# A graph network's gated layer: its steps one longer, three buffers each, and the gathered rows added by VectorE

## The chip, the cores and the metric

The kernel runs on one core of a Trainium2 chip. The metric is the device time of one execution in microseconds (us), the median of several runs. Engines: PE (TensorE), VectorE (DVE), ScalarE (ACT), POOL (GpSimd) and SP (SyncE); the last two mostly issue DMAs.

## The reference

Four graph layers follow one another on 6250 nodes of 128 features, over 106250 edges sorted by the node they point to. Each layer takes `h = relu(layernorm(x))`, and its result is added to `x`: an attention layer, a sum scaled by degrees, a gated layer, and a mean with two weight matrices. The change touches the gated one:

```
x_row, x_col = x[row], x[col]                       # row: source of an edge, col: its target
gates = sigmoid(x_row @ W_src + x_col @ W_dst + edge_attr @ W_edge)
messages = (x_row @ W_msg) * gates
out = segment_sum(messages, col) / maximum(segment_sum(gates, col), 1e-6)
out = out + (x @ W_root + b_root) + x
```

## The kernel before, in words

Edges are cut into tiles of 128 (each tile holds targets of one block of 128 nodes), and four tiles make a group; 220 groups are live. A stage is written as a loop over steps, unrolled by hand, and each engine's program has its own loop with its own offsets: step i of an engine may work on group i for one part and on group i-1 or i-2 for another. Each engine takes its instructions in the order in which they are written, and semaphores tie the engines together. There is no scheduler.

The gated stage, for group q, before the change:

- POOL gathers 128 rows for each tile, four gathers, from the table `tab2` into slot q mod 4 of `G2`. A row holds `x_row @ W_src` (columns 0 to 127) and `x_row @ W_msg` (128 to 255), made in the stage before. From the fifth group on it waits until the product of group q-4 is done (`gated["multiplied"]`), line 820.
- SP loads an index row (`RELROW`, line 910) and four tiles of transposed edge features (`EA`, line 913, a ring of four).
- ScalarE makes from the index row the one-hot rows `ST` (lines 1417, 1419), one step ahead, in two buffers.
- PE, in step q: edge features by `W_edge` (line 1255), one-hot rows by the block's `x_col @ W_dst` (line 1259), and the gathered `x_row @ W_src` added in the same PSUM bank by a product with the identity matrix (line 1263), whose end signals `pre_done`. Then, of group q-1, the aggregation: one-hot matrix `S` by gates and messages `RHS` (line 1047, shared by all layers), signal `agg_done`.
- ScalarE takes the sigmoid of the PSUM bank into `RHS` (line 1426), signal `gate_done`.
- VectorE, in step q: the one-hot matrix `S` of q (line 1579), the product of gates and gathered rows of q-1 (line 2192), signal `multiplied`, and the four additions of q-2 from PSUM into the node sums (line 1598). The index of the block to add to is read into a register first.

Every four groups one block of nodes is finished ("a turn"): VectorE divides, adds and takes moments in a few short instructions, ScalarE takes a square root and normalises the rows, SP stores them.

Of the kernel before, what the change touches and what calls it, by code (L numbers as in the profile page):

```python
# [12 lines left out]
P = 128  # L13
# [8 lines left out]
RING = 4  # L22
DEEP = 8
# [63 lines left out]
def build(nc, sz, a):  # L87
# [4 lines left out]
    with ctx:  # L92
# [333 lines left out]
        hist_in = sem("hist_in")  # L426
        table_made = sem("table_made")
        table_out = sem("table_out")
        srow_in = sem("srow_in")
# [290 lines left out]
        gated = {k: sem(k + "_gated") for k in ("far_known", "st_made", "pre_done", "gate_done", "multiplied")}  # L720
        rel_loaded = [sem(f"rel_loaded{r}") for r in range(2)]
        ea_loaded = [sem(f"ea_loaded{r}") for r in range(RING)]
# [29 lines left out]
        RELROW = SCR[:, 0:512].bitcast(BF16).rearrange("p (r e) -> p r e", r=2)  # L752
        EA = SCR[:, 1024:3072].rearrange("p (r j e) -> p r j e", r=RING, j=QUAD)
# [150 lines left out]
        def sp_edge_rows(sp):  # L904

            def step(i, u):
                q, slot, turn, v = at(i, u, 0)
                if live(q):
                    wait(sp, gated["st_made"], q - 1)
                    sp.dma_start(RELROW[:, v % 2, :], reld.rearrange("(q r) e -> q (r e)", r=QUAD)[bass.ds(q, 1), :]  # L910
                                 .to_broadcast([P, QUAD * P])).then_inc(rel_loaded[v % 2], 16)
                    for j, first in enumerate(registers(sp, SROW, q, sz.edge_end)):
                        sp.dma_start(EA[:, slot, j, :], a["ea_t"][:, bass.ds(first, P)]).then_inc(ea_loaded[slot], 16)
# [3 lines left out]
                due_now = turn_at(i, u, 10)  # L917
# [5 lines left out]
            steps(sp, step, after(10))  # L923
# [52 lines left out]
        def _(sp):  # L976
# [45 lines left out]
            with nc.allow_non_contiguous_dma(reason="single words"):  # L1022
                for m in range(PARTS):
                    run = slice(m * GROUP * sz.chunk, (m + 1) * GROUP * sz.chunk)
                    sp.dma_start(SROW[:, run].rearrange("o (t g) -> o t g", t=GROUP),
                                 metad[1:2, run].rearrange("o (g t) -> o t g", t=GROUP)).then_inc(srow_in, 16)
            sp.wait_ge(srow_in, 16 * PARTS)
# [115 lines left out]
        def _(pe):  # L1143
# [103 lines left out]
            def step(i, u):  # L1247
                q, slot, turn, v = at(i, u, 0)
                if live(q):
# [3 lines left out]
                    pe.wait_ge(ea_loaded[slot], (turn + 1) * 64)  # L1253
                    for j in range(QUAD):
                        nc.tensor.matmul(QD[v % 2][:, j, :], EA[:, slot, j, :], W[:, 4 * D:5 * D], start=j == 0, stop=False,  # L1255
                                         skip_group_check=True)
                    pe.wait_ge(s["st_made"], q + 1)
                    for j in range(QUAD):
                        nc.tensor.matmul(QD[v % 2][:, j, :], ST[:, v % 2, j, :],  # L1259
                                         QT[:, bass.ds(blocks[j], 1), :].rearrange("p o d -> p (o d)"), start=False, stop=False,  # L1260
                                         skip_group_check=True)
# [7 lines left out]
            steps(pe, step, 1)  # L1269
# [6 lines left out]
        def _(act):  # L1276
# [136 lines left out]
            def spread_rows(q, turn, v):  # L1413

                act.wait_ge(rel_loaded[v % 2], (turn + 1) * 16)
                far = RELROW[:, v % 2, :]
                nc.scalar.activation(far, far, ACT.Square, bias=minus_p).then_inc(s["far_known"], 1)
                act.wait_ge(s["far_known"], q + 1)
                nc.scalar.activation(ST[:, v % 2, :, :].rearrange("p j e -> p (j e)"), far, ACT.Relu, bias=1.0, scale=-1.0
                                     ).then_inc(s["st_made"], 1)  # L1420
# [907 lines left out]
```

## Time and profile before

| | |
|---|---|
| runs | 5820.23, 5826.75, 5829.6 us, median 5826.75 |
| profiled execution | 5859.65 us, its span 5858.1 us |
| mean granted clock of TensorE | 0.70 |
| busy over the span | PE 54%, VectorE 53%, ScalarE 23%, POOL 58% |
| DMA | 615.68 MB, mean 105 GB/s |

The span is from the first to the last instruction. Busy shares are averages over stages with different limits: attention, degrees, gated, mean. The gated stage lies between about 3170 and 4610 us. An engine's idle time is put down to the instruction or DMA that released it; "remote" stands where the releaser has no name in the profile, "issue" where the engine waited for nothing that the profile shows.

### The profile page before, as it was taken

To read this page: it belongs to the slowest core of one execution; us is meant where nothing else is said; L and a number is where in the kernel's file an instruction comes from. 1 tells how busy PE (TensorE), PEld (TensorE's weight loads), DVE (VectorE), ACT (ScalarE), POOL (GpSimd) and SP (SyncE) were. 2 spreads that over 40 slices of the span, in tenths; PEclk is the share of its full clock that TensorE was granted. 3 is DMA by queue.
4 is the path that set the end of the run, shared out by engine and by line. 5 is a ranking of instruction groups with operands and counts; after the bars stand their busy time and mean duration, and the time that the engine had idled before them with its cause. 6 is when DMAs were issued, how large, how long until landed. Compare 5 with 4: busy or idle time off the path is not lost.

```text
span 5858.1 us, 61960 instructions
## 1 busy us (share of the span) xinstructions
PE 3148.9 (54%) x15785; PEld 2606.2 (44%) x15785; DVE 3122.3 (53%) x8346; ACT 1366.9 (23%) x2626; POOL 3380.4 (58%) x3531
## 2 busy tenths in 40 slices
PE   6445445454562444444445777777777445433334
PEld 4344444444452333333334666666666334323333
DVE  6556566656676555544444555555555345443334
ACT  2222222222211000001112434434434111111112
POOL 2466556665513666666663555565665466666664
PEclk8666677766775555566767988898998655565555
DMA  3466666666721111112224555555555411111111
GB/s 88 129 172 183 177 184 186 184 187 185 175 60 47 46 46 46 47 52 57 57 57 86 147 143 143 146 146 142 148 147 142 68 48 48 49 49 49 49 48 39
DMA packets 533610, 615.68 MB, mean 105 GB/s; under 512 B 95885, under 2 KB 418126, under 8 KB 533264
## 3 DMA queue, kind: packets, MB, share of 16 engines
q0 software_dynamic: 141168, 347.22, 22.7%
q1 hardware_dynamic: 392096, 264.52, 17.2%
q8 instruction: 136, 2.23, 0.2%
q14 instruction: 210, 1.72, 0.1%
HBM read 527.32 MB, written 84.05 MB: 104 GB/s over the span
## 4 chain that ended last, share of the span: by engine, by line
another core or an unknown queue 26%; DVE 23%; PE 20%; issue 18%; DVEq 5%; ACT 5%; POOL 1%; DMA 1%; SPq 1%; ACTq 0%; POOLq 0%
DVE ACCR L1598 10%; PE PSA L1047 7%; PE PB L1263 3%; PE PB L1255 2%; PE PB L1259 2%; PE PB L615 2%; DVEq L765 2%; DVE SCR L1521 1%; PE PB L1200 1%; ACT FLG L1426 1%; DVEq L1598 1%; DVE S L1579 1%; DVE SCR L2102 1%; DVE FLG L2192 1%
## 5 line engine op out<-in xcount | busy, mean ns | idle before, releaser
L820 POOL DMA_INDIRECT G<-tab,SRC x2640 | 2540.1, 962 | 1784.5 <-issue 765.9
L1598 DVE TENSOR_TENSOR ACCR<-ACCR,PSA 128x128 f32 (+2 forms) x3488 | 1113.9, 319 | 1307.0 <-remote 809.3
L1047 PE MATMUL PSA<-G,S 128*128 128x128 f32 x3326 | 736.8, 390 | 488.1 <-DVE S L1579 283.0
L884 POOL DMA_INDIRECT G<-tab,MV x783 | 741.5, 947 | 384.3 <-issue 221.3
L1047 PEld LDWEIGHTS PSA<-G,S 128*128 128x128 f32 x3326 | 648.7, 289 | 552.0 <-issue 537.5
L1047 PE MATMUL PSA<-FLG,S 128*128 128x256 f32 x1760 | 517.5, 446 | 298.9 <-DVE FLG L2192 268.8
L1047 PEld LDWEIGHTS PSA<-FLG,S 128*128 128x128 f32 x1760 | 373.1, 219 | 503.0 <-DVE FLG L2192 355.1
L1200 PE MATMUL PB<-QTR,ST 128*128 x1792 | 370.6, 370 | 341.9 <-DVE SCR L2089 214.8
L1200 PEld LDWEIGHTS PB<-QTR,ST 128*128 128x128 f32 x1792 | 324.9, 270 | 379.2 <-issue 378.0
L1579 DVE TENSOR_TENSOR S<-PB,REL 128x512 f32<-128x512 f32 x664 | 455.0, 685 | 6.5 <-DMA MV<-mvd 0.7
L2192 DVE TENSOR_TENSOR FLG<-G,FLG 128x512 f32<-128x512 f32 x220 | 151.7, 689 | 465.4 <-ACT FLG L1426 346.4
L1047 PE MATMUL PSA<-SCR,S 128*128 128x137 f32 x1792 | 354.9, 359 | 14.0 <-DVE SCR L2102 14.0
L1047 PEld LDWEIGHTS PSA<-SCR,S 128*128 128x128 f32 x1792 | 331.0, 265 | 23.4 <-DVE SCR L2102 20.6
L1426 ACT ACTIVATE FLG<-PB 128x512 f32<-128x512 f32 x220 | 130.2, 592 | 702.3 <-PE PB L1263 399.2
L1255 PEld LDWEIGHTS PB<-W,SCR 128*128 128x128 f32 x1760 | 275.5, 223 | 39.9 <-issue 16.8
L1121 PE MATMUL PB<-SCR 128*128 128x50 bf16 x880 | 79.0, 216 | 380.7 <-issue 229.4
L1255 PE MATMUL PB<-W,SCR 128*128 128x128 f32 x1760 | 271.4, 304 | 18.2 <-issue 15.2
L1121 PEld LDWEIGHTS PB<-SCR 128*128 128x128 bf16 x880 | 51.2, 115 | 428.2 <-issue 253.9
L1259 PE MATMUL PB<-QTR,ST 128*128 x1760 | 241.0, 281 | 0.0
L1109 PE MATMUL PB<-W,SCR 128*128 128x512 f32 x114 | 95.0, 928 | 248.7 <-ACT SCR L1321 220.1
L1263 PE MATMUL PB<-G,ident 128*128 128x512 f32 x440 | 227.9, 599 | 0.8 <-issue 0.8
L1259 PEld LDWEIGHTS PB<-QTR,ST 128*128 128x128 f32 x1760 | 225.7, 200 | 0.0
(415 smaller groups left out, 4214.5 us busy)
## 6 DMA issues: line engine op xcount, KB each, us to landing
mvd<-G SPq DMA_DIRECT2D x224, 256.0 KB
MV<-mvd SPq DMA_DIRECT2D x224, 256.0 KB
SCR<-in_ea_t SPq DMA_DIRECT2D x880, 64.0 KB
G<-tab,SRC POOLq DMA_INDIRECT x2640
S<-relt SPq DMA_DIRECT2D x224, 128.0 KB
SCR<-reld SPq DMA_DIRECT2D x220, 128.0 KB
G<-tab,MV POOLq DMA_INDIRECT x783
tab<-SCR SPq DMA_DIRECT2D x57, 128.0 KB
```

The costliest lines, as they stand in the source:

```text
L820: nc.gpsimd.indirect_dma_start(out=rows[:, slot, j, :], out_offset=None, in_=table, in_offset=bass.IndirectOffsetOnAxis(ap=SRC[:, k:k + 1] ...
L884: nc.gpsimd.indirect_dma_start(out=whole_rows(q, j), out_offset=None, in_=tab1, in_offset=bass.IndirectOffsetOnAxis(ap=SRCALL[:, k:k + 1], ...
L1047: last = nc.tensor.matmul((PSA if banks is None else banks)[:, par, j, 0:width], S[:, slot, j, :], rhs(j), start=True, stop=True)
L1121: nc.tensor.matmul(HISTP, LOH[:, (2 * v + k) % (2 * RING), j, :], HIH[:, (2 * v + k) % (2 * RING), j, :], start=first, stop=final, skip_gr ...
L1200: last = nc.tensor.matmul(QD[v % 2][:, j, :], ST[:, v % 2, j, :], QT[:, bass.ds(blocks[j], 1), :].rearrange("p o d -> p (o d)"), start=Tru ...
L1255: nc.tensor.matmul(QD[v % 2][:, j, :], EA[:, slot, j, :], W[:, 4 * D:5 * D], start=j == 0, stop=False, skip_group_check=True)
L1259: nc.tensor.matmul(QD[v % 2][:, j, :], ST[:, v % 2, j, :], QT[:, bass.ds(blocks[j], 1), :].rearrange("p o d -> p (o d)"), start=False, sto ...
L1263: nc.tensor.matmul(QD[v % 2], ident[:, :], G2[:, slot, :, 0:D], start=False, stop=True, skip_group_check=True).then_inc(s["pre_done"], 1)
L1426: nc.scalar.activation(RHS[:, v % 2, :, D:2 * D], QD[v % 2], ACT.Sigmoid).then_inc(s["gate_done"], 1)
L1579: return v_.tensor_tensor(S[:, slot, :, :], bc(IOTAP, [P, QUAD, P], 1), rel[:, bass.ds(q * QUAD, QUAD)].unsqueeze(2).to_broadcast([P, QUAD ...
L1598: v_.tensor_tensor(rows, rows, banks[:, par, j, 0:width], ALU.add).then_inc(s["rows_added"], 1)
L2192: v_.tensor_tensor(RHS[:, v % 2, :, 0:D], G2[:, slot, :, D:2 * D], RHS[:, v % 2, :, D:2 * D], ALU.mult).then_inc(s["multiplied"], 1)
```

## The change

The loops of the gated stage get one step more. PE's three products become two: the gathered rows no longer go through PE. VectorE adds them, in place, to the finished PSUM bank, as the first thing of its step, and the sigmoid reads the sum from `G2`. The buffers between the engines are three instead of two (PSUM banks, one-hot rows, gates and messages), the ring of edge features has three slots instead of four, the one of gathered rows keeps its four. Index rows lie in four buffers and are loaded two groups ahead. The aggregation of a group comes two steps after its products, the additions three steps after. VectorE puts the first of the four additions ahead of the one-hot matrix, and the product last. The work of a turn moves by one step.

```diff
 # SP
-                    wait(sp, gated["st_made"], q - 1)
-                    sp.dma_start(RELROW[:, v % 2, :], ...)
+                if live(q + 2):
+                    index_rows(q + 2)                   # waits for st_made, q - 1
+                    wait(sp, gated["pre_done"], q - 2)
                     for j, first in enumerate(registers(sp, SROW, q, sz.edge_end)):
-                        sp.dma_start(EA[:, slot, j, :], ...)
+                        sp.dma_start(EA[:, q % THIRD, j, :], ...)
 # PE
+                    pre, spread = GQD[q % THIRD], GSTS[q % THIRD]
-                    pe.wait_ge(ea_loaded[slot], (turn + 1) * 64)
+                    pe.wait_ge(ea_loaded[q % THIRD], (q // THIRD + 1) * 64)
...
-                    pe.wait_ge(ps[3]["gathered"][slot], (turn + 1) * 64)
-                    nc.tensor.matmul(QD[v % 2], ident[:, :], G2[:, slot, :, 0:D], start=False, stop=True,
-                                     skip_group_check=True).then_inc(s["pre_done"], 1)
-                q, slot, turn, v = at(i, u, -1)
+                    last.then_inc(s["pre_done"], 1)
+                q, slot, turn, v = at(i, u, -2)
                 if live(q):
                     pe.wait_ge(s["multiplied"], q + 1)
-                    pe_agg(pe, 3, q, slot, v % 2, lambda j: RHS[:, v % 2, j, :], 2 * D)
+                    wait(pe, ps[3]["rows_added"], (q - 1) * QUAD)
+                    both = gated_rhs(q)
+                    pe_agg(pe, 3, q, q % THIRD, v % 2, lambda j: both[:, j, :], 2 * D)
 # ScalarE
-                    act.wait_ge(s["pre_done"], q + 1)
-                    nc.scalar.activation(RHS[:, v % 2, :, D:2 * D], QD[v % 2], ACT.Sigmoid).then_inc(s["gate_done"], 1)
+                    act.wait_ge(s["summed"], q + 1)
+                    nc.scalar.activation(gated_rhs(q)[:, :, D:2 * D], G2[:, slot, :, 0:D], ACT.Sigmoid).then_inc(s["gate_done"], 1)
 # VectorE
                 q, slot, turn, v = at(i, u, 0)
                 if live(q):
-                    onehot(3, q, slot)
+                    sums = G2[:, slot, :, 0:D]
+                    dve.wait_ge(ps[3]["gathered"][slot], (turn + 1) * 64)
+                    dve.wait_ge(s["pre_done"], q + 1)
+                    v_.tensor_tensor(sums, sums, GQD[q % THIRD], ALU.add).then_inc(s["summed"], 1)
+                q, slot, turn, v = at(i, u, -3)
+                add = row_adder(3, acc2, 2 * D, q, v % 2)
+                add(0)
+                q = at(i, u, 0)[0]
+                if live(q):
+                    onehot(3, q, q % THIRD)
+                for j in range(1, QUAD):
+                    add(j)
...
```

VectorE's instructions in the middle of the stage, before. L1579 is the one-hot matrix, L2192 the product, L1598 an addition to the node sums (ISA computes its address):

```order
L1579 TENSOR_TENSOR S<-PB0,REL 128x512 [waits dve_step_gated]
L2192 TENSOR_TENSOR FLG<-G,FLG 128x4x128 [waits gate_done_gated]
L765 TENSOR_LOAD BROW [waits rows_added_gated]
L1598 ISA [waits agg_done_gated]
L1598 TENSOR_TENSOR ACCR<-ACCR,PSA 128x256
L1598 ISA [waits rows_added_gated]
```

The same place after the change. L2214 is the new addition of the gathered rows, L1621 an addition to the node sums, L1602 the one-hot matrix, L2227 the product:

```order
L2214 TENSOR_TENSOR G<-G,PB1 128x4x128 [waits pre_done_gated,gathered2_gated]
L777 TENSOR_LOAD BROW [waits rows_added_gated]
L1621 ISA [waits agg_done_gated]
L1621 TENSOR_TENSOR ACCR<-ACCR,PSA 128x256
L1602 TENSOR_TENSOR S<-PB0,REL 128x512
L1621 ISA [waits rows_added_gated]
L1621 TENSOR_TENSOR ACCR<-ACCR,PSA 128x256
...
L2227 TENSOR_TENSOR SCR<-G,SCR 128x4x128 [waits gate_done_gated]
```

The one instruction that waits for PE's `pre_done` now stands at the head of VectorE's step, ahead of the product of the group before; formerly ScalarE waited for it.

PE's instructions in the middle of the stage, before; L1255 are the products of edge features, L1259 those of the one-hot rows, L1263 the identity product, L1047 the aggregation:

```order
L1255 MATMUL PB1<-W,SCR 128x128 [waits ea_loaded2]
L1255 MATMUL PB1<-W,SCR 128x128 x3
L1259 ISA [waits st_made_gated]
L1259 MATMUL PB1<-QTR,ST 128x128
...
L1263 MATMUL PB1<-G,ident 128x512 [waits gathered2_gated]
L1047 MATMUL PSA<-FLG,S 128x256 [waits multiplied_gated]
L1047 MATMUL PSA<-FLG,S 128x256 x3
```

And after, with L1277 and L1281 for the products and L1068 for the aggregation, now that of the group two back:

```order
L1277 MATMUL PB1<-W,SCR 128x128 [waits ea_loaded0]
L1277 MATMUL PB1<-W,SCR 128x128 x3
L1281 ISA [waits st_made_gated]
L1281 MATMUL PB1<-QTR,ST 128x128
...
L1068 MATMUL PSA<-FLG,S 128x256 [waits rows_added_gated,multiplied_gated]
L1068 MATMUL PSA<-FLG,S 128x256 x3
```

PE waits no longer for gathered rows, and its aggregation waits in addition for VectorE's additions of a group further back.

## Rows read from the trace of the kernel before

**Rows 1.** The page's chain of waits, shares of the span by engine.
```profile
another core or an unknown queue 26%; DVE 23%; PE 20%; issue 18%; DVEq 5%; ACT 5%; POOL 1%; DMA 1%; SPq 1%; ACTq 0%; POOLq 0%
```

**Rows 2.** Line 2192, the product of the gated layer; nanoseconds min/median/max.
```profile
L2192 DVE TENSOR_TENSOR FLG<-G,FLG x220: 679/692/736, 3183.4 to 4604.1; 128x512 f32<-128x512 f32 x110
```

**Rows 3.** Busy time in two stretches; columns: microseconds, then engines, PEclk, DMA share, GB/s.
```profile
3190.00:4600.00 1410.00, 1111.24 (x5629) 888.68 (x5628) 784.90 (x1786) 571.28 (x865) 826.31 (x860) 0.90 0.55 144
...
3645.00:3647.00 2.00, 1.42 (x3) 1.18 (x4) 1.69 (x4) 1.95 (x3) 0.94 (x1) 0.58 0.00 0
```

**Rows 4.** Timeline of one repeat; start us, us, engine, line, [idle before <-releaser].
```profile
3631.05 0.60 ACT L1426 ACTIVATE FLG<-PB 128x512 f32<-128x512 f32 x1 [2.54 <-PE PB L1263]
...
3632.43 1.99 PE L1047 MATMUL PSA<-FLG,S 128*128 128x256 f32 x8 [1.40 <-DVE FLG L2192]
3632.65 0.94 POOL L820 DMA_INDIRECT G<-tab,SRC  x1 [3.34 <-DVE FLG L2192]
3632.83 0.58 ACT L1426 ACTIVATE FLG<-PB 128x512 f32<-128x512 f32 x1
...
3633.90 2.27 SPq L913 DMA_DIRECT2D SCR<-in_ea_t  x4
...
3635.15 1.05 POOL L820 DMA_INDIRECT G<-tab,SRC  x1 [0.30 <-issue]
...
3636.05 1.02 PE L1263 MATMUL PB<-G,ident 128*128 128x512 f32 x2
...
3636.62 2.10 DVE L1598 TENSOR_TENSOR ACCR<-ACCR,PSA 128x256 f32 x4
...
3636.93 5.78 SPq L913 DMA_DIRECT2D SCR<-in_ea_t  x4
...
3638.63 1.05 PE L1255 MATMUL PB<-W,SCR 128*128 128x128 f32 x8
...
3640.42 1.02 PE L1263 MATMUL PB<-G,ident 128*128 128x512 f32 x2
3641.59 0.95 POOL L820 DMA_INDIRECT G<-tab,SRC  x1 [0.30 <-issue]
3644.20 0.60 ACT L1426 ACTIVATE FLG<-PB 128x512 f32<-128x512 f32 x1 [9.52 <-remote]
...
3644.83 0.69 DVE L2192 TENSOR_TENSOR FLG<-G,FLG 128x512 f32<-128x512 f32 x1 [4.36 <-ACT FLG L1426]
...
3645.44 2.10 DVE L1598 TENSOR_TENSOR ACCR<-ACCR,PSA 128x256 f32 x4
...
3645.58 3.54 PE L1047 MATMUL PSA<-FLG,S 128*128 128x256 f32 x8 [4.13 <-DVE FLG L2192]
3645.79 0.94 POOL L820 DMA_INDIRECT G<-tab,SRC  x1 [3.26 <-DVE FLG L2192]
```

**Rows 5.** Waits from 3190 to 4600 us: total us, times, longest.
```profile
ACT FLG L1426 <- PE PB L1263: 393.8, 71, 9.6
...
POOL G L820 <- DVE FLG L2192: 313.1, 101, 3.8
ACT FLG L1426 <- remote: 281.4, 42, 9.6
```

**Rows 6.** Timeline of the last layer, same columns.
```profile
5010.52 1.10 PE L1086 MATMUL PB<-QTR,ST 128*128 x4
...
5014.54 1.09 PE L1086 MATMUL PB<-QTR,ST 128*128 x4
...
5018.99 0.95 POOL L884 DMA_INDIRECT G<-tab,MV  x1 [0.30 <-issue]
5020.36 0.29 DVE L1481 TENSOR_TENSOR ACCR<-ACCR,PB 128x128 f32 x1 [5.15 <-remote]
```

**Rows 7.** Groups by line and form, 3190 to 4600 us; busy us, mean ns.
```profile
L1579 DVE TENSOR_TENSOR S<-PB,REL 128x512 f32<-128x512 f32 x217 | 149.6, 689 | 5.6
L2192 DVE TENSOR_TENSOR FLG<-G,FLG 128x512 f32<-128x512 f32 x216 | 148.9, 689 | 441.5 <-ACT FLG L1426 322.6 <-issue 118.9
```

More of the change, by code:

```diff
@@ L719, in build @@
         hist_ready = sem("hist_ready")
-        gated = {k: sem(k + "_gated") for k in ("far_known", "st_made", "pre_done", "gate_done", "multiplied")}
-        rel_loaded = [sem(f"rel_loaded{r}") for r in range(2)]
-        ea_loaded = [sem(f"ea_loaded{r}") for r in range(RING)]
+        gated = {k: sem(k + "_gated") for k in ("far_known", "st_made", "pre_done", "summed", "gate_done", "multiplied")}
+        rel_loaded = [sem(f"rel_loaded{r}") for r in range(4)]
+        ea_loaded = [sem(f"ea_loaded{r}") for r in range(THIRD)]
         mixed = {k: sem(k + "_degree") for k in ("dve_step", "factors", "spread_out", "rows_normed", "turned", "copied", "multiplied", "staged",
@@ L922, in step @@
                     sp.dma_start(tab1[bass.ds(b * P, P), :], line_of(H, b)).then_inc(rows_stored, 16)
-            steps(sp, step, after(10))
+            sp.wait_ge(ps[2]["agg_done"], LIVE)
+            for q in range(2):
+                index_rows(q)
+            steps(sp, step, after(11))
         def sp_results(sp):
@@ L1025, in _ @@
                     sp.dma_start(SROW[:, run].rearrange("o (t g) -> o t g", t=GROUP),
[L1026 to L1027 removed]
+                                 metad[1:2, run].rearrange("o (g t) -> o t g", t=GROUP)).then_inc(hist_in, 16)
+            sp.wait_ge(hist_in, 16 + 16 * PARTS)
             sp.wait_ge(turns_in, 32)
@@ L1252, in step @@
                     blocks = registers(pe, BROW, q, NB)
-                    pe.wait_ge(ea_loaded[slot], (turn + 1) * 64)
+                    pre, spread = GQD[q % THIRD], GSTS[q % THIRD]
+                    pe.wait_ge(ea_loaded[q % THIRD], (q // THIRD + 1) * 64)
                     for j in range(QUAD):
-                        nc.tensor.matmul(QD[v % 2][:, j, :], EA[:, slot, j, :], W[:, 4 * D:5 * D], start=j == 0, stop=False,
+                        nc.tensor.matmul(pre[:, j, :], EA[:, q % THIRD, j, :], W[:, 4 * D:5 * D], start=j == 0, stop=False,
                                          skip_group_check=True)
@@ L1438, in step @@
                                          scale=TS[:, r, 8:9]).then_inc(settled["rows_normed"], 1)
-            spread_rows(0, 0, 0)
-            steps(act, step, after(4))
+            for q in range(2):
+                spread_rows(q)
+            steps(act, step, after(5))
             act.wait_ge(settled["rows_normed"], TURNS_ALL)
@@ L2187, in step @@
                 if live(q):
-                    onehot(3, q, slot)
+                    sums = G2[:, slot, :, 0:D]
[10 more added lines that the diff above has]
+                    add(j)
                 q, slot, turn, v = at(i, u, -1)
                 if live(q):
+                    both = gated_rhs(q)
                     dve.wait_ge(s["gate_done"], q + 1)
-                    v_.tensor_tensor(RHS[:, v % 2, :, 0:D], G2[:, slot, :, D:2 * D], RHS[:, v % 2, :, D:2 * D], ALU.mult).then_inc(s["multiplied"], 1)
-                q, slot, turn, v = at(i, u, -2)
-                add = row_adder(3, acc2, 2 * D, q, v % 2)
-                for j in range(QUAD):
-                    add(j)
-                now = turn_at(i, u, 4)
+                    v_.tensor_tensor(both[:, :, 0:D], G2[:, slot, :, D:2 * D], both[:, :, D:2 * D], ALU.mult).then_inc(s["multiplied"], 1)
+                now = turn_at(i, u, 5)
                 if now:
@@ L2200, in step @@
                     turn_factors(chain(t, GATE_SPREAD), s_, t, r)
-                now = turn_at(i, u, 0)
+                now = turn_at(i, u, 1)
                 if now:
@@ L2208, in step @@
                     c_(v_.reciprocal(both[:, D:2 * D], both[:, D:2 * D]))
-                now = turn_at(i, u, 1)
+                now = turn_at(i, u, 2)
                 if now:
@@ L2218, in step @@
                     c_(v_.tensor_tensor(x_row, x_row, both[:, 0:D], ALU.add))
-                now = turn_at(i, u, 2)
+                now = turn_at(i, u, 3)
                 if now:
@@ L2227, in step @@
                     turn_stats(c_, s_, line_of(X, b), r)
-            steps(dve, step, after(4))
+            steps(dve, step, after(5))
             dve.wait_ge(ps[3]["rows_added"], LIVE * QUAD)
```

50 lines of the change are left out of this document (30 added, 20 removed).

## Prediction

> **What bounds the kernel now.** I read the page's chain first. Its largest share, 26%, has no engine's name: it is a wait for something the profile can't see [rows 1]. The change touches one stage, the gated layer, so I then read that stage: line by line, its waits, and one repeat of its pattern in the timeline. Its 220 products on VectorE start between 3183.4 and 4604.1 us, so a group of four tiles takes 1420.7 / 219 = 6.49 us [rows 2]. No engine is full there: in 1410 us PE is busy for 1111, POOL for 826, VectorE for 785, ScalarE for 571 us, and PE is granted 0.90 of its clock [rows 3]. POOL is nearest to a floor. A gather takes 0.95 us and the next follows 0.30 us later, so four take 5.0 us, 1.5 us less than a group lasts [rows 4]. The rest is POOL's wait for the product that frees a slot, 313 us in 101 waits [rows 5].
>
> What is late in front of that product? The sigmoid. It waits for the identity product 71 times (393.8 us) and 42 times (281.4 us) for the unnamed thing [rows 5]. Take three groups a, b, c of the repeat. The sigmoid of a starts at 3631.05, of b at 3632.83, of c at 3644.20. The identity product of c is recorded from 3636.05 to 3637.07, and that of the next group at 3640.42, but the sigmoid of c starts 7.1 us after the first of these ended. What precedes it is the end of the gathers: POOL runs eight from 3632.65 to 3642.54, and 1.66 us later the sigmoid starts [rows 4]. The last layer has no identity product and shows the same: products of line 1086 are recorded at 5010.52 and 5014.54, POOL's gathers end at 5019.94, and VectorE gets a result at 5020.36 after 5.15 us idle, again from an unnamed releaser [rows 6]. I read it so: while gathered rows flow, what PE has finished becomes known late, mostly when POOL has run out of permitted gathers and its data are in. What ends before the flow is known at once: the aggregation recorded from 3632.43 to 3634.42, 1.8 us after POOL's start, was in VectorE's additions at 3636.62 [rows 4].
>
> That makes the stage a row of rounds of two groups: 9.89 us of gathers, 1.66 us until the signals come, 1.59 us for sigmoid, product and POOL's next start (3645.79), together 13.15 us (3631.05 to 3644.20) [rows 4]. Half of it is 6.57 us; the stage's mean was 6.49.
>
> **The change part by part.** *The identity product goes*: 1.02 us by 220, 224 us of PE's time [rows 4]. PE stands idle for 4.13 us before the aggregation at 3645.58 as it is [rows 4], so this is worth nothing on the path, which runs through the signal.
>
> *VectorE adds the gathered rows*, one 128x512 operation a group. The trace has not this form, but a 128x512 operation takes 0.689 us with an operand in PSUM (line 1579) and with both in SBUF (line 2192) [rows 7]. So 0.69 us, 152 us in all, for an engine with 625 us free [rows 3]. What matters is its place. It stands first in a step and waits for PE's signal and the gathered rows. Behind it are queued the four additions of the group three back, the one-hot, and the product of the group before. So the product of group q, which needed PE's signal of q, now also needs that of q+1.
>
> *The ring of gathered rows keeps four slots*, still freed by the product. With signals known up to group m, POOL could gather up to m+4, and now up to m+3. The third buffers don't change that, since PE's aggregation still waits for the product, two groups back in place of one.
>
> *The new round.* Let the signals come at T. VectorE does the new addition (0.61 us to the next start, as from 3644.83 to 3645.44), four additions (2.10), the one-hot (0.61) and the product (0.69), 4.01 us. POOL starts 0.27 us after a product, so at T+4.28, where it was T+1.59. The next product follows about 4 us on, before POOL has done its four gathers. The third addition then needs PE's next signal. PE starts the aggregation in front of it at T+4.0, after a longer idle time than now, and after 4.13 us of idle time the granted clock was 0.58 and the aggregation took 3.54 us in place of 1.99 [rows 3, 4]. The two operand products take 1.79 us at full clock (3638.63 to 3640.42) [rows 4]. They end at T+9.3, 5.0 us after POOL's start. The identity product of c ended 4.4 us after it and stayed unknown to the end of the flow. So again two groups a round: 4.28 + 9.89 + 1.66 = 15.83 us, 7.91 us a group.
>
> *Sum.* 110 rounds by 15.83 - 13.15 = 2.68 us give +295 us, and the extra step +8 us. The profiled execution took 5859.65 us, so 6163 us. That execution stands 33 us above the median of the runs shown: 6130 us.
>
> *The rest.* SP now waits for PE's signal of three groups back before it loads edge columns. Four issues take 2.27 us outside the flow and 5.78 us in it [rows 4]. At T it has two groups to issue, about 6 us, and the flow begins about then; they are needed a round later. I take 0, with POOL's and VectorE's 10 us of round as cover; without that cover 3.5 us a round. Index rows further ahead lie on ScalarE, which has 839 us free [rows 3]: 0, from -5 to +5 us. Gathers beside VectorE's work: at 3635.15 one took 1.05 us where 0.95 is usual [rows 4], so 220 more operations cost between 0 and 22 us, and I take 0, because the addition stands where POOL is idle. The Trainium skill (Perfetto Trace Analysis, Optimizing Scalar/DVE Operations) says that GpSimd and VectorE share an SBUF read port, which speaks against one more tensor operation on VectorE; the 0.10 us fits it.
>
> **The rivals.** *Three groups a round.* If PE's signal still gets through, VectorE goes on to a third product: 4.28 + 3 x 4.98 + 1.66 = 20.9 us, 6.96 us a group, (6.96 - 6.57) x 220 = +86 and +8: 5921 us. For it: the rows bound the last good moment only between 1.8 and 4.4 us after POOL's start, and at full clock the products would end 3.5 us after it. Against it: the half clock.
>
> *The lag belongs to the identity product.* It alone reads the gathered rows on PE, and in the flow it may be slow or end later than recorded. Then the change removes the lag, and POOL (5.0 us a group) or VectorE (785 / 1410 x 6.49 = 3.61 us busy, 0.69 more, and its short waits) sets the pace: at best 220 x (6.49 - 5.0) = 328 us less, and with a fifth of it lost to clock and turns 260 us less: 5567 us. For it: 394 of the sigmoid's 675 us of waiting name that product [rows 5]. Against it: the last layer waits likewise for other products [rows 6], and the next identity product is recorded as started at 3640.42, in order behind one that would be running still. The Trainium skill (Perfetto Trace Analysis, Tensor Engine Instruction) says that the end shown for TensorE is estimated from the instruction's size and not observed; by that rule the product of c may have ended only at 3644.20, and this rival would hold. The trace agrees only so far that the recorded end did not release ScalarE.
>
> *SP takes POOL's place.* As the last, but in an unbroken flow SP needs 5.78 us and some 0.8 for the index row, 6.6 us a group: about +0.1 x 220, 5850 us.
>
> **How the numbers follow.** Two groups a round 0.50 (own range 6040 to 6200: down if a third of the rounds take three groups, up by the 22 us and late loads), three groups 0.20, lag removed 0.22, SP 0.08. The time is that of the first. A measurement of this kernel can tell about 0.2% from no change. Slower: 0.50 + 0.20 + 0.02 of SP's = 0.72. Faster: 0.22 + 0.01. Same: 0.05, the rest of SP's. The range reaches from the first case over the second and the fourth: 5800 to 6200. It leaves out the removed lag.
>
> **What would show it.** Right: POOL idle for 5 to 6 us between runs of eight gathers (3.3 us now), the new addition as the instruction that waits for an unnamed releaser, a lower mean clock of PE, the stage near 1735 us. Runs of twelve gathers would show the second case. Wrong: hardly a pause of POOL beyond its 0.30 us, and the new addition waiting for gathered rows and not for PE. Then the lag hung on the identity product.

## The result

The changed kernel takes 5857.73 us (median of six, 5847.59 to 5872.47), the one before 5824.02 us (median of six, 5818.02 to 5829.6). The ratio is 1.0061, 95% interval 1.0044 to 1.0078: slower by 0.6%, 34 us. I had forecast slower by 303 us.

The profiled execution has a span of 5870.6 us. Its products in the gated stage, line 2227 now, come in two forms (the third buffer has another name):

```profile
L2227 DVE TENSOR_TENSOR FLG<-G,FLG x147: 678/684/727, 3150.8 to 4620.9; 128x512 f32<-128x512 f32 x147
L2227 DVE TENSOR_TENSOR SCR<-G,SCR x73: 682/684/727, 3166.2 to 4617.0; 128x512 f32<-128x512 f32 x73
```

From the first to the last are 1470.1 us, 6.71 us a group, where it was 6.49 [rows 2]. That is 49 us for the stage, near the 34 us of the medians. The profiled execution of before lay 33 us above its median, and it was late already ahead of the stage: its first gather of the stage starts at 3160, that of the changed kernel at 3126 us. So the two are compared by the stage, not by their spans.

Busy times, columns as in [rows 3]:

```profile
3190.00:4600.00 1410.00, 975.96 (x5045) 855.27 (x5043) 855.55 (x1948) 564.39 (x844) 808.20 (x843) 0.84 0.56 139
```

PE lost the identity products (1111 to 976 us), VectorE got the additions (785 to 856), and the granted clock fell from 0.90 to 0.84. The new addition takes what I had put down (687 ns), and waits as I had said, half of the time for an unnamed releaser. Of the rows shown the first and the third are its waits, the other two are POOL's waits for the product. Line and releaser, total us, times, longest:

```profile
DVE G L2214 <- remote: 228.7, 59, 8.7
POOL G L832 <- DVE FLG L2227: 214.2, 70, 6.3
...
DVE G L2214 <- PE PB L1281: 196.9, 41, 6.4
...
POOL G L832 <- DVE SCR L2227: 134.0, 36, 6.3
```

POOL's two rows are 348 us in 106 waits, longest 6.3, where they were 313 in 101, longest 3.8 [rows 5]. So its longest waits are far longer, as forecast, but there are too few of the long ones. The unnamed releaser isn't the addition's own gathered rows: at the begin of 48 of the 56 stops of POOL over 2.5 us in which an addition starts, POOL had already gathered two groups past the one that is added, and one or three in the other eight. One repeat of the new pattern, four groups in 27.2 us; the timeline's columns are those of [rows 4]:

```profile
3865.32 0.83 PE L1281 MATMUL PB<-QTR,ST 128*128 x6
...
3865.86 0.95 POOL L832 DMA_INDIRECT G<-tab,SRC  x1 [1.26 <-DVE FLG L2227]
...
3866.29 0.69 DVE L2214 TENSOR_TENSOR G<-G,PB 128x512 f32<-128x512 f32 x1
...
3873.11 0.69 DVE L2214 TENSOR_TENSOR G<-G,PB 128x512 f32<-128x512 f32 x1 [2.36 <-remote]
...
3877.05 0.94 POOL L832 DMA_INDIRECT G<-tab,SRC  x1 [1.26 <-issue]
...
3880.80 0.95 POOL L832 DMA_INDIRECT G<-tab,SRC  x1 [0.30 <-issue]
3881.60 0.27 PE L1281 MATMUL PB<-QTR,ST 128*128 x1 [0.92 <-issue]
3883.14 0.69 DVE L2214 TENSOR_TENSOR G<-G,PB 128x512 f32<-128x512 f32 x1 [6.36 <-PE PB L1281]
...
3886.13 0.68 DVE L2227 TENSOR_TENSOR FLG<-G,FLG 128x512 f32<-128x512 f32 x1
...
3886.87 3.78 PE L1068 MATMUL PSA<-FLG,S 128*128 128x256 f32 x8 [5.00 <-DVE FLG L2227]
...
3887.09 0.94 POOL L832 DMA_INDIRECT G<-tab,SRC  x1 [5.34 <-DVE FLG L2227]
...
3888.11 0.95 DVE L2239 RECIPROCAL ACCR<-ACCR  x1
...
3889.10 0.69 DVE L2214 TENSOR_TENSOR G<-G,PB 128x512 f32<-128x512 f32 x1
...
3890.84 0.94 POOL L832 DMA_INDIRECT G<-tab,SRC  x1 [0.30 <-issue]
3892.09 0.68 DVE L2227 TENSOR_TENSOR SCR<-G,SCR 128x512 f32<-128x512 f32 x1
3892.15 1.24 PE L1281 MATMUL PB<-QTR,ST 128*128 x8
...
3893.04 0.94 POOL L832 DMA_INDIRECT G<-tab,SRC  x1 [1.26 <-DVE SCR L2227]
```

Read it from the long stop. PE's products end at 3881.87, POOL's last permitted gather at 3881.75, and the addition starts at 3883.14, 1.39 us after that gather. The product is at 3886.13, and POOL starts after 5.34 us. Up to here this is the forecast round. But POOL now has leave for four gathers only, since each product frees the rows of one group. They end at 3891.78, VectorE's next product starts at 3892.09, and POOL stops again, for 1.26 us. PE's next result ends at 3893.39, 0.35 us after POOL has restarted, and its addition runs at once (one repeat earlier: PE's end at 3866.15, the addition at 3866.29). Then come eight gathers, in which one more result gets through, late and midway (3873.11). The pattern is common: of 38 stops over 5 us that another stop follows, 34 are followed by exactly four gathers and a stop of 1.2 to 1.35 us.

The table is worked out from the starts and ends of the 880 gathers of the stage in each trace: stage is from the first to the last, stops are POOL's idle times of over 0.45 us between two of them. The ratio is to the kernel before, timed in turn with the run. Compare ratios, not microseconds, since the level of the same kernel differs from one set of runs to another: before took 5880 us beside the four runs stops5 to soon_stops4, and 5822 to 5830 us beside all others.

| kernel | median us | ratio, 95% interval | stage us | stops, sum us | over 2.5 us |
|---|---|---|---|---|---|
| before | 5824.0 | | 1422 | 347 | 95 |
| changed | 5857.7 | 1.0061 (1.0044 to 1.0078) | 1475 | 406 | 65 |
| add_alone | 6036.2 | 1.0356 (1.0329 to 1.0384) | 1652 | 615 | 154 |
| longer_alone | 5861.7 | 1.0063 (1.0042 to 1.0084) | 1473 | 390 | 62 |
| product_first | 5945.3 | 1.0209 (1.0183 to 1.0235) | 1570 | 495 | 69 |
| product_soon | 5912.4 | 1.0149 (1.0124 to 1.0174) | 1512 | 441 | 106 |
| half_rows | 5869.7 | 1.0069 (1.0046 to 1.0091) | 1471 | 403 | 72 |
| few_edge_loads | 5881.7 | 1.0089 (1.0062 to 1.0115) | 1483 | 402 | 54 |
| no_edge_products | 5870.6 | 1.0069 (1.0045 to 1.0092) | 1471 | 394 | 55 |
| longer_product_first | 5821.1 | 0.9982 (0.9967 to 0.9997) | 1436 | 360 | 77 |
| stops (eight memsets) | 5916.7 | 1.0163 (1.0146 to 1.018) | 1527 | 483 | 0 |
| half_gathers | 5409.5 | 0.9288 (0.9271 to 0.9304) | 1023 | 539 | 84 |
| add_twice | 5864.7 | 1.0058 (1.0036 to 1.0081) | 1477 | 410 | 90 |
| stops5 | 5856.0 | 0.9962 (0.9945 to 0.9979) | 1416 | 355 | 1 |
| stops3 | 5835.4 | 0.9917 (0.9887 to 0.9946) | 1393 | 353 | 34 |
| before_stops4 | 5804.6 | 0.9868 (0.9842 to 0.9893) | 1361 | 309 | 0 |
| soon_stops4 | 5806.4 | 0.987 (0.9843 to 0.9898) | 1360 | 309 | 0 |
| before_stops3 | 5746.0 | 0.9849 (0.9812 to 0.9887) | 1348 | 300 | 15 |
| before_stops2 | 5787.6 | 0.9933 (0.991 to 0.9956) | 1386 | 336 | 42 |
| soon_stops3 | 5756.0 | 0.9873 (0.9834 to 0.9912) | 1353 | 292 | 11 |

The two first rows hold the account in short. The stage is 53 us longer, and POOL's stops are 59 us longer in sum. The long stops hardly changed in sum: 95 of 3.2 us on average are 302 us, 65 of 4.8 us are 310. What was added are short stops, 45 us before and 97 after, mostly of the 1.3 us just shown (61 of them).

### The profile page after: what moved, and what is told of

Read it like the earlier page. It is cut to its first block and busy times, and to the rows that moved or that the text cites. A ratio compares the mean times of both kernels' runs of the same rounds, so it can differ in the third digit from the quotient of the medians.

```text
span 5870.6 us, 61739 instructions
## 1 busy us (share of the span) xinstructions
PE 3051.3 (52%) x15345; PEld 2607.1 (44%) x15345; DVE 3219.3 (55%) x8566; ACT 1375.0 (23%) x2626; POOL 3371.1 (57%) x3531
## 5 line engine op out<-in xcount | busy, mean ns | idle before, releaser
L1621 DVE TENSOR_TENSOR ACCR<-ACCR,PSA 128x128 f32 (+2 forms) x3488 | 1110.3, 318 | 1200.3 <-remote 760.4
L1068 PE MATMUL PSA<-G,S 128*128 128x128 f32 x3326 | 744.1, 393 | 554.9 <-DVE S L1602 351.2
L1068 PEld LDWEIGHTS PSA<-G,S 128*128 128x128 f32 x3326 | 655.3, 292 | 626.5 <-issue 613.7
L1068 PE MATMUL PSA<-SCR,S 128*128 128x137 f32 (+1 forms) x2376 | 555.0, 394 | 164.7 <-DVE SCR L2227 110.1
L1068 PEld LDWEIGHTS PSA<-SCR,S 128*128 128x128 f32 x2376 | 469.8, 261 | 209.3 <-DVE SCR L2227 118.4
L1221 PE MATMUL PB<-QTR,ST 128*128 x1792 | 368.0, 369 | 333.4 <-DVE SCR L2112 203.9
L1068 PE MATMUL PSA<-FLG,S 128*128 128x256 f32 x1176 | 365.6, 465 | 240.6 <-DVE FLG L2227 175.6
L1221 PEld LDWEIGHTS PB<-QTR,ST 128*128 128x128 f32 x1792 | 324.5, 270 | 370.1 <-issue 368.9
L1602 DVE TENSOR_TENSOR S<-PB,REL 128x512 f32<-128x512 f32 x664 | 453.6, 683 | 2.3 <-DMA MV<-mvd 2.1
L2214 DVE TENSOR_TENSOR G<-G,PB 128x512 f32<-128x512 f32 x220 | 151.0, 687 | 491.1 <-remote 267.1
L1068 PEld LDWEIGHTS PSA<-FLG,S 128*128 128x128 f32 x1176 | 258.0, 230 | 303.0 <-DVE FLG L2227 190.3
L1277 PEld LDWEIGHTS PB<-W,SCR 128*128 128x128 f32 x1760 | 288.8, 232 | 72.3 <-DMA SCR<-in_ea_t 31.7
L1277 PE MATMUL PB<-W,SCR 128*128 128x128 f32 x1760 | 287.8, 314 | 53.4 <-DMA SCR<-in_ea_t 30.2
L1281 PE MATMUL PB<-QTR,ST 128*128 x1176 | 174.7, 291 | 18.8 <-issue 18.5
L2112 DVE TENSOR_TENSOR SCR<-G,PB 128x512 f32<-128x512 f32 x224 | 152.4, 681 | 56.9 <-remote 34.1
L1402 ACT COPY SCR<-SCR 128x32 f32<-128x32 f32 x224 | 48.8, 218 | 572.1 <-remote 363.1
L1281 PEld LDWEIGHTS PB<-QTR,ST 128*128 128x128 f32 x1176 | 159.9, 208 | 28.2 <-issue 28.1
```

What stands on the lines that cost most here:

```text
L1068: last = nc.tensor.matmul((PSA if banks is None else banks)[:, par, j, 0:width], S[:, slot, j, :], rhs(j), start=True, stop=True)
L1221: last = nc.tensor.matmul(QD[v % 2][:, j, :], ST[:, v % 2, j, :], QT[:, bass.ds(blocks[j], 1), :].rearrange("p o d -> p (o d)"), start=Tru ...
L1277: nc.tensor.matmul(pre[:, j, :], EA[:, q % THIRD, j, :], W[:, 4 * D:5 * D], start=j == 0, stop=False, skip_group_check=True)
L1281: last = nc.tensor.matmul(pre[:, j, :], spread[:, j, :], QT[:, bass.ds(blocks[j], 1), :].rearrange("p o d -> p (o d)"), start=False, stop= ...
L1602: return v_.tensor_tensor(S[:, slot, :, :], bc(IOTAP, [P, QUAD, P], 1), rel[:, bass.ds(q * QUAD, QUAD)].unsqueeze(2).to_broadcast([P, QUAD ...
L1621: v_.tensor_tensor(rows, rows, banks[:, par, j, 0:width], ALU.add).then_inc(s["rows_added"], 1)
```

## The experiments

### The two parts, and VectorE's order

**add_alone**: the kernel before with the new addition in place of the identity product.

```diff
+                    dve.wait_ge(ps[3]["gathered"][slot], (turn + 1) * 64)
+                    dve.wait_ge(s["pre_done"], q + 1)
+                    v_.tensor_tensor(sums, sums, QD[v % 2], ALU.add).then_inc(s["summed"], 1)
                     onehot(3, q, slot)
```

> The kernel before with one part of the change: the identity product goes, VectorE adds the gathered rows at the head of its step. Steps, buffers and rings stay as before. Theory A (stops): PE's finished work becomes known only when the gathered rows stop flowing, and the change was saved from my 6130 us because three buffers let PE be ahead, and because VectorE's longer queue makes POOL stop briefly more often, in which stops signals pass. With two buffers PE's products of q+1 wait for the product of q-1, which now waits for PE's signal of q: one signal for each group, at 4.3 + 4.7 us or more. So far slower than both, 6300 to 6500 us. Theory B (relief): the new addition costs little and the relief of PE pays for it: 5800 to 5900 us.

6036 us, ratio 1.0356. Its direction was theory A's, its size neither's: POOL gathers in fours (216 runs of four), with 3.0 to 3.5 us between half of them (108). The addition alone costs six times what the whole change costs, so with it in place the longer steps pay most of it back.

**longer_alone**: the changed kernel with the identity product back and no new addition.

```diff
+                    pe.wait_ge(ps[3]["gathered"][slot], (turn + 1) * 64)
+                    nc.tensor.matmul(pre, ident[:, :], G2[:, slot, :, 0:D], start=False, stop=True, ...)
-                    v_.tensor_tensor(sums, sums, GQD[q % THIRD], ALU.add).then_inc(s["summed"], 1)
```

> The changed kernel with the identity product put back on PE and the new addition left out: only the longer steps, the third buffers and the index rows further ahead. Theory A: the product of a group doesn't need the signal of the next one, so the long stop of POOL is 3.2 us again as before, and a third bank lets three signals pass in one stop: between before and 90 us less, 5740 to 5825 us. Theory B: nothing of the gain is in the buffers, PE's work is back: 5825 us or more, up to 5870.

5862 us: theory A missed, the number is theory B's. Three groups do pass in a stop (35 of 62 long rounds have twelve gathers), as A said. But the stop is most often 5.7 us (5.4 on average), since VectorE's additions and one-hot stand ahead of the product in this order too. And a second thing shows, PE's own timeline within the run of gathers:

```profile
3717.13 0.27 PE L1277 MATMUL PB<-W,SCR 128*128 128x128 f32 x1
3717.85 0.48 PE L1277 MATMUL PB<-W,SCR 128*128 128x128 f32 x2 [0.45 <-issue]
3719.26 0.39 PE L1277 MATMUL PB<-W,SCR 128*128 128x128 f32 x2 [0.93 <-issue]
3720.71 0.27 PE L1277 MATMUL PB<-W,SCR 128*128 128x128 f32 x1 [1.05 <-issue]
3722.11 0.27 PE L1277 MATMUL PB<-W,SCR 128*128 128x128 f32 x1 [1.14 <-issue]
```

Matmuls that take 0.13 us elsewhere (eight in 1.05) come singly, and PE waits for nothing named. With the weight loads between them, starts are 0.70 us apart. I count, from 3190 to 4600 us, neighbouring starts among all of PE's records, its sequencer's too, that are 0.6 to 0.8 us apart: 10 in the kernel before, 205 in the changed one (130 us), 421 here (292 us). Among matmuls and weight loads alone there are 10, 74 and 397. So PE is itself held where it runs further ahead.

**product_first** and **product_soon**: the changed kernel with VectorE's product of the group before ahead of the addition, or the product of the same group right behind addition and one-hot.

```diff
 # product_first: a step is
+    product(q - 1); addition(q); adds(q - 3)[0]; onehot(q); adds(q - 3)[1:]
 # product_soon
+    addition(q); onehot(q); product(q); adds(q - 3)
```

> The changed kernel with VectorE's product of q-1 ahead of the new addition of q, so that it doesn't wait for PE's signal of q. Theory A as I sized it in the prediction (the wait for the next group's signal is what costs): POOL gets its group of lead back, 5780 to 5840 us. Theory A with stops that let signals pass: the short stops of 1.3 us go, and with them the signals that pass in them, so little or nothing is gained: 5840 to 5900 us. Theory B: no change, 5858 us.

> The changed kernel with another order on VectorE: addition of q, one-hot of q, product of q (the one-hot covers the sigmoid), then the four additions to the node sums. A signal now leads to the product's end 2.1 us later, not 4.0. Theory A: the long stop of POOL falls from 5.3 to about 3.7 us, some 60 to 110 of them: 100 to 180 us less, 5680 to 5760 us. Theory B (the pace is not set by what follows the signal): 5858 us.

In product_soon ScalarE's sigmoid also moves one step forward, to the group that has just been added. 5945 and 5912 us: both are slower than the changed kernel, by 1.5% and 0.9%, though one takes the wait for the next group's signal off the product, and the other takes work out from between signal and product. Theory A as I had it falls; only its variant in the third expectation (short stops carry signals, and go) has the right direction, and it too was passed. product_first doesn't shorten the way from a group's addition to its product, for the additions, the one-hot and the work of a turn still lie between. In this stop they are 5.18 us:

```profile
3710.03 0.69 DVE L2219 TENSOR_TENSOR G<-G,PB 128x512 f32<-128x512 f32 x1 [9.02 <-remote]
...
3715.21 0.69 DVE L2213 TENSOR_TENSOR FLG<-G,FLG 128x512 f32<-128x512 f32 x1
...
3716.18 0.94 POOL L832 DMA_INDIRECT G<-tab,SRC  x1 [8.68 <-DVE FLG L2213]
```

It has 60 rounds of twelve gathers with 6.5 us of stop each, and 495 us of stops where the changed kernel has 406. In product_soon the signal at 3712.6 leads to POOL's start 2.35 us later, as meant:

```profile
3710.06 0.95 POOL L832 DMA_INDIRECT G<-tab,SRC  x1 [0.30 <-issue]
...
3712.61 0.69 DVE L2214 TENSOR_TENSOR G<-G,PB 128x512 f32<-128x512 f32 x1 [3.41 <-remote]
...
3714.96 0.94 POOL L832 DMA_INDIRECT G<-tab,SRC  x1 [3.95 <-DVE FLG L2221]
```

But it has 100 rounds of eight gathers with a stop of 4.1 us each, where the changed kernel has mostly twelve to twenty gathers to a long stop. Against before, where 75 rounds of 95 are of two groups too, each stop is 0.9 us longer (3.2 there); a hundred times that is 90 us, and 90 were measured (5912.4 - 5822.3). In both variants the sum of the stops accounts for the time. How many groups pass between two stops decides as much as their length; that product_soon's order is what lowered it is argued from the trace, not tested.

### What holds PE's signals

**half_rows**, **few_edge_loads**, **no_edge_products**: the changed kernel with half the bytes of the gathered rows; with SP's edge features loaded for three groups only, and PE's wait for them to match; without PE's products of edge features. All three compute something else than the layer. The edits in short, in the gated stage alone:

```diff
 # half_rows
-                        out=rows[:, slot, j, :], in_=table,
+                        out=rows[:, slot, j, 0:D], in_=table.rearrange("n (h d) -> (n h) d", h=2),
 # few_edge_loads
+                    for j, first in enumerate(...) if q < THIRD else ():
 # no_edge_products
-                        nc.tensor.matmul(pre[:, j, :], EA[:, q % THIRD, j, :], W[:, 4 * D:5 * D], ...)
```

> The changed kernel, whose 880 gathers of the gated stage fetch 128 of a row's 256 columns, so half the bytes by the same number of instructions (the messages then use stale columns, and the gates wrong rows). Theory A: what holds PE's signals back are the gathered rows on their way. With half of them the signals get through while POOL gathers, the stops go: 150 to 350 us less, 5500 to 5700 us. Theory C: POOL's issuing of gathers holds them back, whatever it fetches: 5830 to 5880 us.

> The changed kernel, in which SP loads edge features for the first three groups only (later groups use these again), so 256 KB less a group beside the 512 KB of gathered rows and 128 KB of index rows. Theory A with any transfer counting: signals pass sooner, 5650 to 5800 us. If only the gathered rows count: 5830 to 5880 us.

> The changed kernel without PE's products of edge features by their weights (the gates lack that term; SP still loads the features): 16 of some 48 loads and products of PE a group are gone. Theory A as seen in the runs so far (in the flow PE's instructions come through one in 0.70 us, once enough of them stand in line, and signals stand in that line): fewer instructions, signals earlier, 100 to 250 us less, 5610 to 5760 us. If it is only PE's time, which waits for the product anyway: 5830 to 5870 us.

5870, 5882 and 5871 us: theory A predicted less time in each, by 58 us at the least, and none came. The row of half_rows beside that of the changed kernel shows 100 GB/s in place of 139 and all else as it was:

```profile
3190.00:4600.00 1410.00, 971.67 (x5024) 848.30 (x5022) 851.03 (x1942) 562.00 (x839) 803.91 (x840) 0.83 0.46 100
```

So it is not the bytes in flight, not SP's loads, and not PE's number of instructions. What is left is POOL's own issuing of gathers, the expectations' theory C, tested next.

**longer_product_first**: longer_alone with the product first in VectorE's step.

```diff
 # a step is
+    product(q - 1); adds(q - 3)[0]; onehot(q); adds(q - 3)[1:]
```

> The longer steps and third buffers with the identity product on PE (as in the second run), and VectorE's product of q-1 first in its step, so that after a signal only sigmoid and product come before POOL's next start. Theory A: the long stop of POOL falls from 5.7 back to 3.2 us, at three groups a round: 70 to 130 us less than the second run's 5862, so 5730 to 5790 us, unless PE, further ahead, is held back more (then 5800 to 5950 us, with more of PE's instructions 0.70 us apart).

5821 us, 0.7% less than longer_alone, level with the kernel before to slightly below it (0.9982). Most stops are back to 3 to 4 us (46), but PE is held as feared (319 starts 0.7 us apart, 222 us), with stops of up to 8 us. It came out above the range of 5730 to 5790, and in that of the second case (PE held back more, 5800 to 5950).

**half_gathers**, **add_twice** and **stops**: two gathers a group in place of four; the new addition made twice; and eight small memsets on POOL, each waiting for the one before, behind each group's gathers. In half_gathers the addition waits for two gathers, not four.

```diff
 # half_gathers
-                for j in range(QUAD):
+                for j in range(2 if n == 3 else QUAD):
 # add_twice
+                    v_.tensor_tensor(gated_rhs(q)[:, :, 0:D], G2[:, slot, :, 0:D], GQD[q % THIRD], ALU.add)
 # stops
+                if n == 3:
+                    for k in range(8):
+                        nc.gpsimd.memset(st2[:, :], 0.0).then_inc(reordered, 1)
+                        pool.wait_ge(reordered, 8 * q + k + 3)
```

> The changed kernel with eight small memsets in a chain behind each group's four gathers, some 1.6 us of work for POOL that nobody needs, 350 us in all. Theory C (after the run with half the bytes: PE's signals are held while POOL issues gathers, and pass in a stop of about 2 us): each group gets a stop in which its signals pass, the long stops go, and a group takes 5.0 + 1.6 to 2.0 us: 5800 to 5950 us, about no change. If signals pass no more easily in such stops, POOL's added work adds to its path: 6100 to 6250 us.

> The changed kernel with two gathers a group in the gated stage in place of four (the other two tiles of a slot keep old rows): the same half of the bytes as in the run with half rows, but half of the instructions too. Theory C: POOL's part of each round halves, 2.5 us a group less, until PE, VectorE and the stops bound it: 5350 to 5600 us. If the stops alone set the round (signals take their time whatever POOL does): 5750 to 5860 us.

> The changed kernel with the new addition made twice (the first result is thrown away), 0.61 us more for VectorE between signal and product. Theory C: it lengthens each of some 58 long stops by 0.61 us, and the shorter ones that wait for a product too, together 35 to 85 us: 5893 to 5943 us. If VectorE is off the path: 5858 us.

Half the gathers (the other half of each slot keeps old rows): 5409 us, 448 less than the changed kernel, where half the bytes had given nothing. PE's clock is 0.96 there (3190 to 4100 us). It doesn't show what holds the signals, though. The gathers themselves take 428 us less in sum (845 to 417) and the 0.30 us between two of them some 150 us less, while POOL's stops grew from 406 to 539 us: what was gained is POOL's own time. The run that bears on it is the one with eight memsets. They are 1.54 us a group and 339 us in all for POOL, and the kernel takes 5917 us, only 59 more. Its trace has no stop over 2.5 us; what POOL waits for is no longer a product:

```profile
POOL G L832 <- issue: 184.7, 566, 2.1
POOL G L832 <- POOL st L838: 110.6, 189, 0.9
```

Both times are within theory C's ranges. The doubled addition missed: 5865 us, 7 more than the changed kernel and within the measurement, where 35 to 85 were expected. Its stops fell into another pattern, 56 of them of 3 to 4 us and 13 over 5, instead of 3 and 39. It runs in 72 rounds of two groups with 3.6 us of stop. The stops don't simply grow by what is put between signal and product.

### How long a stop the signals need

The same memsets, fewer, in the changed kernel, in the kernel before and in product_soon. The edit is that of stops, with 5, 3, 4 and 4 in place of 8, and in the second set 3, 2 and 3.

> The changed kernel with five of the small memsets behind each group's four gathers in place of eight, so a stop of some 1.55 us where eight gave 2.1. If a stop of this length still lets the signals pass, POOL alone sets the pace at 4.7 + 1.55 us a group, 0.46 us less than the changed kernel's 6.71: 101 us less, 5757 us. If it is too short, the long stops come back on top: 5860 to 5950 us.

> The same with three memsets, a stop of some 1.2 us, as short as those in which signals seldom passed in the traces so far. If it does for them: 4.7 + 1.2 = 5.9 us a group, 5680 us. If not, as those traces say: long stops again and 5850 to 5950 us. I expect the second.

> The kernel before with four of these memsets behind each group's four gathers, a stop of some 1.35 us. If such stops let the identity product's signal pass, a group takes 4.7 + 1.35 = 6.05 us where it took 6.49: 5728 us. If not, 0.8 us of POOL's work per group add to rounds of two groups, or vanish in POOL's idle time: 5830 to 5950 us.

> The fourth run's kernel (product right behind addition and one-hot, 5912 us) with four memsets, a stop of some 1.35 us. Its chain from signal to product is the shortest with the new addition, so it needs POOL's lead least. If the stops let signals pass: 6.05 us a group, 5710 us. If not: 5900 to 6000 us.

> The kernel before with three memsets, a stop of some 1.2 us behind each four gathers (four gave 1.35 us and no long stop at all). If signals still pass: 4.7 + 1.2 = 5.9 us a group and 0.2 us less than with four, 40 us: about 2.0% below the kernel before. If not: long stops of 3 us again, level with the kernel before or slower.

> The same with two memsets, a stop of some 1.0 us. Where the traces had such stops, signals seldom passed in them (12 of 39 times). I expect the long stops back and 0 to 1% below the kernel before; if signals pass, 5.7 us a group and 2.8% below it.

> The fourth run's kernel (the new addition, product right behind it) with three memsets in place of four, a stop of some 1.2 us. If signals pass: 40 us less than with four, about 2.0% below the kernel before; if the chain from signal to product (0.7 us longer here than with the identity product) is too long for POOL's lead by then, stops longer than 1.2 us return and it is level with four memsets.

With four memsets the kernel before has 219 stops of 1.0 to 1.5 us, one behind each group, and none over 2.5; it takes 1.3% less. POOL's waits and the stage's row, to set beside [rows 5] and [rows 3] (here up to 4500 us):

```profile
POOL G L820 <- issue: 308.8, 806, 2.1
POOL G L820 <- POOL st L826: 22.7, 39, 0.6
```

```profile
3190.00:4500.00 1310.00, 1040.18 (x5512) 835.31 (x5511) 784.26 (x1751) 566.01 (x851) 942.03 (x1690) 0.94 0.59 152
```

The wait for the product, 313 us, is gone. What PE waits for now is the gathered rows themselves (PE's line and releaser, total us, times, longest), a wait that the kernel before does not have in that stretch:

```profile
PE PB L1267 <- DMA G<-tab,SRC: 255.6, 137, 4.2
```

Stops of 1.2 us leave 15 long ones in the kernel before, 34 in the changed one and 11 in product_soon; stops of 1.0 us leave 42 in the kernel before. Three memsets in the kernel before are the fastest of all that do the whole layer, 5746 us against 5830 beside it, ratio 0.9849 (0.9812 to 0.9887): it beats the kernel before by 1.5% and the changed one by about 2.1% (0.9849 / 1.0061, from two sets of runs). Three and four memsets can't be told apart (the intervals overlap), nor can the kernel before and product_soon with equal stops. With such stops the change, in product_soon's order, is worth nothing and costs nothing. Of my expectations, before_stops4 (5728 us, reckoned for a kernel before of 5826, so 0.983) and before_stops3 (0.98) were near, those of soon_stops4 (0.980 expected, 0.987 measured) and stops5 too hopeful (0.988 expected, 0.996 measured: one long stop only, but 6.43 us a group for 6.25), that of stops3 too gloomy. Part of the gap is that a group takes a little more than 4.7 us and its stop: 6.19 us with four memsets, where the sum is 6.05. before_stops2 (0.7% below, the long stops back) is what I expected, and soon_stops3 (1.3% below, seven stops of 4 us) is its second case.

## Why the prediction was wrong

The sign was right, the size nine times too large: 295 us for the stage, 49 to 53 measured. That 5858 us lies within 5800 to 6200 is luck: the forecast's own case had 6040 to 6200, and the case of SP in POOL's place, whose 5850 us is nearest, has the wrong mechanism (without SP's loads the kernel took 5882 us).

**Right: the chain behind a signal.** I had T+4.28 for POOL's start; it is 3887.09 - 3883.14 = 3.95 us, with POOL idle 5.34 us. The addition takes 687 ns for 689 taken. PE's clock after the idle time: the aggregation took 3.78 us for 3.54 taken, and the stage's clock fell from 0.90 to 0.84. PE's third result I had at T+9.3; it ends at T+10.25. Gathers beside VectorE's additions at 0: a gather took 0.960 us on average against 0.961. SP's new wait at 0 fits few_edge_loads, which gained nothing; the index rows at 0 were not tested.

**Wrong: "the next product follows about 4 us on, before POOL has done its four gathers", and with it "5.0 us after POOL's start" and "again two groups a round".** The next product came 5.96 us on, because the group that ends a block brings VectorE short work I had left out of this sum (the reciprocal alone 0.95 us). It missed the end of POOL's four gathers by 0.3 us. So POOL stopped once more, and PE's result, later than I had it, fell 0.35 us behind the restart, where by the prediction's own reading a signal is known at once. Instead of two groups to each long stop four pass in this repeat, in 27.2 us (6.80 a group). I summed 110 long stops in both kernels; the traces have 95 over 2.5 us before and 65 after, with 13 gathers from one to the next on average. Nor do the forecast's two halves go together: 30 of the 65 follow sixteen gathers, with 5.3 us on average, and only 13 follow eight, with 3.5. That the work of a turn is what makes the product late is read off the trace; no run took it away. Eleven unbroken runs of twelve gathers were seen, the sign I had named for the second rival, whose 6.96 us a group is nearer than my 7.91; but its mechanism, a third product without a stop, isn't the common one.

**Wrong in the picture: "while gathered rows flow".** Half the bytes changed nothing (5870), and a pause of POOL with all bytes unchanged removed the long waits. What holds PE's signals goes with POOL's unbroken gathering. Whether it is the gathers' number or that of the rows they name isn't told apart: half_rows kept both, and half_gathers, which halves both, gained no more than POOL's own time. The Trainium skill (DMA: Bandwidth & Descriptors, SWDGE vs HWDGE vs iDMA) says that GpSimd computes each descriptor in software and writes it to rings in SBUF before a DMA engine moves a byte. The traces agree only so far that halving the bytes left a gather at 0.957 us; that these writes stand in the signals' way is argued, not shown.

**The rival that the identity product causes the lag** falls: without it signals are as late (228.7 us of the addition's wait has no name). That the change's two parts don't add up was in none of my cases: the addition alone costs 3.6%, the longer steps in the same order 0.6%, both together 0.6%.

## What stays open

Why PE's signals wait for POOL isn't settled. Each timed execution reports a span and a clock, so all were recorded in some form. The Trainium skill (NOTIFIC — the notification-queue block, Overflow: three behaviours, one of which stalls the engine) says that the block that writes such records can, in one of its settings, stall the engine that makes them when the ring for them is full. No run here shows whether that setting was on or the ring full; if they were, PE's starts 0.70 us apart and part of the stops would belong to the recording. Nor is it shown which of the memsets' effects counts, the pause alone or also the steadier rhythm it gives PE.

## What to carry to other kernels

A sum over rounds needs two numbers, what a stop costs and how many groups pass in one; here the first was right to 0.3 us where it was read, and the second was wrong (110 long stops summed, 65 found), where the repeat shows a margin of 0.3 us between two engines. Where a stage alternates between long runs and long stops, a regular short stop can be faster than none (1.5% here): before shortening a chain, try to slow the engine that runs ahead. A change that hangs on such a rhythm should be forecast with the patterns next to it, not with one.

## What the runs showed of the hardware

- PE's finished work became known to VectorE and ScalarE mostly after POOL's last gather of a run: in stops over 2.5 us 1.7 us after it before the change, 1.4 after it, and 1.0 to 2.2 in the other kernels (medians). In nine of the first ten traces (all but no_edge_products), of the results that by PE's recorded end stood unanswered when a stop of POOL began, 16 of 55 were answered within 2.6 us where the stop was 1.25 us long (rounded to quarters), 17 of 23 at 2.0 us, and 525 of 645 from 3 us up. A regular stop of 1.35 us behind each four gathers was enough.
- Half the bytes of 880 gathers: no change in time (5870 us against 5858, the intervals overlap) and none in a gather's 0.96 us.
- PE held to a start each 0.70 us while POOL gathered on: 292 us of such spacing in longer_alone, 7 in the kernel before.
- Four memsets behind each group, 0.75 us by 220 or 165 us of work for nothing on the gathering engine, took 1.3% off the kernel.
